# Window scan layer: two of the eight step-size products of a tile move from GpSimd to VectorE, with new order tables

## The reference

```python
dt = jax.nn.silu(dt_raw @ dt_W + dt_b)
a = -jnp.exp(A_log)
dA = jnp.exp(dt[..., None] * a)
dBx = dt[..., None] * b_st[:, :, None, :] * x[..., None]
def step(state, inp):
    dA_t, dBx_t, c_t = inp
    state = dA_t * state + dBx_t
    y = jnp.einsum('bcn,bn->bc', state, c_t)
```

## Time and profile before

| | us |
|---|---|
| median of three runs | 4724.54 |
| lowest and highest | 4721.48, 4733.52 |
| the profiled execution: time | 4733.78 |
| its span (first to last instruction) | 4732.0 |
| TensorE busy | 4400.7 (93%) |
| VectorE busy | 3875.3 (82%) |
| GpSimd busy | 3672.9 (78%) |
| ScalarE busy | 3347.4 (71%) |

### The profile page before, as it was taken

One profiled execution on the slowest core, in us unless ns is written; L12 is line 12 of the kernel. 1 busy time (PEld: TensorE's weight loads), 2 busy tenths in 40 slices (PEclk: granted clock), 3 DMA queues, 4 the chain that ended last, 5 costly groups with the idle time before them and its releaser, 6 DMA issues. The chain is left out here.

```text
span 4732.0 us, 79417 instructions
## 1 busy us (share of the span) xinstructions
PE 4400.7 (93%) x24320; PEld 3136.2 (66%) x24320; DVE 3875.3 (82%) x7295; ACT 3347.4 (71%) x5828; POOL 3672.9 (78%) x3476
## 2 busy tenths in 40 slices
PE   3799999999999999999998799999999999999998
PEld 2465656565656565656555478877778787878887
DVE  2899999999999999999999477777777777777775
ACT  3888898889898889888986255555555555555555
POOL 1989898989898989989898267766666676666666
PEclk7899999999999999999999799999999999999999
DMA  2011111111111111111111400031001300040000
GB/s 76 12 49 33 49 34 49 33 49 33 49 38 45 38 45 38 44 38 45 40 42 41 129 13 22 21 97 43 22 21 28 105 22 20 22 120 19 16 20 19
DMA packets 139268, 198.15 MB, mean 42 GB/s; under 512 B 18346, under 2 KB 106388, under 8 KB 138644
## 3 DMA queue, kind: packets, MB, share of 16 engines
q1 hardware_dynamic: 138900, 193.76, 12.9%
HBM read 114.02 MB, written 79.69 MB: 41 GB/s over the span
## 5 line engine op out<-in xcount | busy, mean ns | idle before, releaser
L1273 POOL TENSOR_TENSOR pl<-probs,ph 128x512 fp32r<-128x512 f32 x1024 | 1322.2, 1292 | 649.6 <-PE ps_o L1383 322.1
L742 POOL TENSOR_TENSOR dec<-dt,rates 128x384 f32<-128x384 f32 x1536 | 1512.9, 1015 | 285.2 <-ACT dt L628 229.6
L1476 ACT ACTIVATE ph<-ps_s 128x512 fp32r<-128x512 f32 x1024 | 612.7, 598 | 908.3 <-PE ps_s L1366 900.7
L1488 DVE TENSOR_REDUCE part_max<-ps_m 128x1 f32<-128x512 f32 x1024 | 687.4, 688 | 394.4 <-PE ps_m L1349 394.3
L1375 PE MATMUL ps_o<-ph,vh 128*128 128x512 f32 x2048 | 813.4, 397 | 17.6 <-ACT o_ch L1462 17.3
L1375 PE MATMUL ps_o<-ph,vl 128*128 128x512 f32 x2048 | 806.5, 394 | 0.0
L1517 DVE TENSOR_TENSOR ps_a<-probs,ps_a 128x512 f32<-128x512 f32 x992 | 681.3, 687 | 40.8 <-ACT probs L1478 35.3
L1383 PE MATMUL ps_o<-pl,vh 128*128 128x512 f32 x2048 | 635.1, 391 | 0.0
L1478 ACT ACTIVATE probs<-ps_s 128x512 f32<-128x512 f32 x1024 | 607.3, 593 | 0.0
L900 DVE SCALAR_TENSOR_TENSOR psS<-u,bc,psS 128x384 f32<-128x384 f32 x1024 | 597.3, 611 | 1.2
L909 DVE SCALAR_TENSOR_TENSOR y_tok<-psS,bc,y_tok 128x384 f32<-128x384 f32 x960 | 552.3, 604 | 4.5
(11 more groups left out here) (166 smaller groups left out, 7671.8 us busy)
## 6 DMA issues: line engine op xcount, KB each, us to landing
values_d<-hid SPq DMA_DIRECT2D x64, 512.0 KB, 4.3
xf<-in_x_dram SPq DMA_DIRECT2D x128, 128.0 KB
xb<-in_x_dram SPq DMA_DIRECT2D x128, 128.0 KB
residual_d<-xb SPq DMA_DIRECT2D x32, 512.0 KB, 2.6
vh<-values_d SPq DMA_DIRECT2D x32, 512.0 KB, 7.4
vl<-values_d SPq DMA_DIRECT2D x32, 512.0 KB, 9.1
res<-residual_d SPq DMA_DIRECT2D x32, 512.0 KB, 3.3
out_dram<-res SPq DMA_DIRECT2D x128, 128.0 KB
```

The lines of the kernel that those rows point to most:

```text
L742: last = nc.gpsimd.tensor_tensor(dec[:, q % RING, j - 1, :], dt[:, par, d, token_of(d, j), :], rates[:, d, n, :], ALU.mult)
L1273: nc.gpsimd.tensor_tensor(pl[:, m % DEPTH, :], probs[:, m % DEPTH, :], ph[:, m % DEPTH, :].bitcast(F32), ALU.subtract).then_inc(pl_ok, 1)
L1476: nc.scalar.activation(ph[:, m % DEPTH, :], ps_s[m % 2][:, :], ACT.Exp).then_inc(ph_ok, 1)
L1488: nc.vector.tensor_reduce(part_max[:, qt, kc:kc + 1], ps_m[r % 2][:, :], AX.X, ALU.max).then_inc(max_out, 1)
```

## The change

Three things. The products `umb2` and `umb3` are taken out of `POOL_ORDER` and put into `DVE_ORDER`, after st17 and after st22, where a new function `multiply` issues them as a tensor_tensor on VectorE. They count on a semaphore of their own, `u_dve`; `multiplied` counts GpSimd's six alone, and each reader of the backward products, and each step that overwrites an input, waits for both. And all four tables get a new order. Among what moves: on TensorE, out1 before conv0a, h2t0 before xnt0, w12 before pw2, inx2 to inx4 between w20 and w21, inx5 before dt2, the two x1t behind dt2, bct behind v1; on ScalarE, ow before exp2, z2 and exp4 before ln1_norm, exp6 before xnt0, inx1 and dt0 before exp12, exp0 to the end; on VectorE, w20 behind st35 and w21 behind st41; on GpSimd, acc13 before arg0, acc14 before umf3. The readers that are left out of the diff below change in the same way as those shown.

```diff
--- before.py
+++ after.py
@@ -38,26 +38,25 @@
 
 
 PE_ORDER = """
-    z0 z1 yt0- yt1- yt2- z2 out0- conv0a out1- conv1a conv2a conv0b conv0c conv1c conv2c xnt0+ h2t0- h2t1- xnt1+
-    pw0 w10- xnth+ pw1 w11- proj+ pw2 inx0+ w12- inx1+ w13- inx2+ dtf0+ dtb0+ w20- inx3+ w21- dtf1+ dtb1+ inx4+
-    x1t0- dtf2+ dtb2+ x1t1- inx5+ dtf3+ dtb3+ fg0- xk0+ xk1+ xk2+ v0- bct+ v1-
+    z0 z1 yt0- yt1- yt2- z2 out0- out1- conv0a conv1a conv2a conv0b conv0c conv1c conv2c h2t0- xnt0+ h2t1- xnt1+
+    pw0 xnth+ w10- pw1 w11- proj+ w12- pw2 inx0+ w13- inx1+ dtf0+ dtb0+ w20- inx2+ inx3+ inx4+ w21- dtf1+ dtb1+
+    inx5+ dtf2+ dtb2+ x1t0- x1t1- dtf3+ dtb3+ fg0- xk0+ xk1+ xk2+ v0- v1- bct+
 """.split()
 ACT_ORDER = """
-    exp1 ln1_std+ exp2 ow exp3 z0 z1 ln1_norm+ z2 exp4 ln2_std- exp5 ln2_norm- conv0c conv1c conv2c xnt0+ exp6
-    h2t0- h2t1- xnt1+ exp7 exp8 pw0 w10- xnth+ pw1 w11- exp9 proj+ exp10 pw2 inx0+ w12- inx1+ w13- exp11 inx2+
-    exp12 dtf0+ dtb0+ exp13 inx3+ exp14 dtf1+ dtb1+ inx4+ x1t0- dtf2+ dtb2+ x1t1- inx5+ dtf3+ dtb3+ exp15 fg0-
-    xk0+ xk1+ xk2+ exp0+ v0- bct+ v1-
+    exp1 ln1_std+ ow exp2 exp3 z0 z1 z2 exp4 ln1_norm+ ln2_std- exp5 ln2_norm- conv0c conv1c conv2c exp6 h2t0-
+    xnt0+ h2t1- xnt1+ exp7 exp8 pw0 xnth+ w10- pw1 w11- exp9 proj+ exp10 w12- pw2 inx0+ w13- exp11 inx1+ dtf0+
+    dtb0+ exp12 inx2+ inx3+ exp13 inx4+ exp14 dtf1+ dtb1+ inx5+ dtf2+ dtb2+ x1t0- x1t1- dtf3+ dtb3+ exp15 fg0-
+    xk0+ xk1+ xk2+ v0- v1- bct+ exp0+
 """.split()
 DVE_ORDER = """
-    st0 ln1_stats+ st1 ln1_mean+ st2 yt0- st3 yt1- st4 ln1_rstd+ st5 yt2- st6 ln1_shift+ st7 st8 st9 out0- st10
-    out1- ln2_stats- ln2_mean- st11 st12 ln2_rstd- st13 ln2_shift- st14 st15 st16 st17 st18 st19 st20 st21 st22
-    st23 st24 st25 st26 st27 st28 st29 st30 st31 st32 st33 st34 st35 st36 st37 st38 st39 w20- w21- st40 st41
-    st42 st43 st44 st45 fg0- st46 st47 gd_mul+ v0- gd_sum+ v1-
+    st0 ln1_stats+ st1 ln1_mean+ st2 yt0- st3 st4 ln1_rstd+ yt1- st5 yt2- st6 ln1_shift+ st7 st8 out0- st9 st10
+    out1- ln2_stats- ln2_mean- st11 st12 ln2_rstd- st13 ln2_shift- st14 st15 st16 st17 umb2 st18 st19 st20 st21
+    st22 umb3 st23 st24 st25 st26 st27 st28 st29 st30 st31 st32 st33 st34 st35 w20- st36 st37 st38 st39 st40
+    st41 w21- st42 st43 st44 st45 fg0- st46 st47 gd_mul+ v0- gd_sum+ v1-
 """.split()
 POOL_ORDER = """
-    arg2 arg3 umb0 acc0 arg4 acc1 arg5 umb1 umb2 acc2 arg6 acc3 arg7 acc4 arg8 umb3 acc5 arg9 acc6 arg10 acc7
-    arg11 acc8 arg12 acc9 arg13 acc10 arg14 acc11 arg15 acc12 arg0+ acc13 umf0+ umf1+ umf2+ umf3+ acc14 acc15
-    arg1+
+    arg2 arg3 acc0 arg4 acc1 umb0 arg5 umb1 acc2 arg6 acc3 arg7 acc4 arg8 acc5 arg9 acc6 arg10 acc7 arg11 acc8
+    arg12 acc9 arg13 acc10 arg14 acc11 arg15 acc12 acc13 arg0+ umf0+ umf1+ umf2+ acc14 umf3+ acc15 arg1+
 """.split()
 RATES_BEFORE = "proj"
 
@@ -196,9 +195,13 @@
     return state_op(k, q, op) if q >= 0 else state_op(k - 1, q + CHAINS, op)
 
 
-def multiplied(f, d, t):
-
-    return 2 * T * f + T * d + t + 1
+U_BY_DVE = [step for step, at in map(target, DVE_ORDER) if step.startswith("um")]
+U_BY_POOL = 2 * T - len(U_BY_DVE)
+
+
+def multiplied(f, d):
+
+    return U_BY_POOL * f + (T if d == 0 else U_BY_POOL)
 
 
 def token_of(d, j):
...
@@ -623,7 +627,9 @@
                 elif job.startswith("dt"):
                     d, t = "fb".index(job[2]), int(job[3])
                     if t == 0 and f > 1:
-                        act.wait_ge(u_mul, multiplied(f - 2, d, T - 1))
+                        act.wait_ge(u_mul, multiplied(f - 2, d))
+                        if d == 1:
+                            act.wait_ge(u_dve, len(U_BY_DVE) * (f - 1))
                         act.wait_ge(arg_ok, CHAINS * (f - 2) + STATES * (d + 1))
                     last = nc.scalar.activation(dt[:, par, d, t, :], bank[:, 0:INNER], ACT.Silu)
                 elif job.startswith("z"):
...
@@ -793,8 +800,19 @@
                                                           ALU.mult, ALU.mult)
                 last.then_inc(ok, 1)
 
+            def multiply(f, step, par):
+
+                d, t = "fb".index(step[2]), int(step[3])
+                dve.wait_ge(front_out, front_job(f, "dtb3"))
+                dve.wait_ge(front_out, front_job(f, "xk2"))
+                if f > 0:
+                    dve.wait_ge(state_ok, TILE_OPS * f)
+                nc.vector.tensor_tensor(u[:, d, t, :], dt[:, par, d, t, :], x_win[:, t, :], ALU.mult).then_inc(u_dve, 1)
+
             def front(step, f, par):
-                if step.startswith("ln1") and step != "ln1_std":
+                if step.startswith("um"):
+                    multiply(f, step, par)
+                elif step.startswith("ln1") and step != "ln1_std":
                     if step == "ln1_stats":
                         dve.wait_ge(x_loaded, 96 * (f + 1))
 
...
@@ -880,7 +899,9 @@
                             if not (exact(k) and k < 2):
                                 dve.wait_ge(back_full, back_job(k - 2, "yt2"))
                         if q % STATES == 0:
-                            dve.wait_ge(u_mul, multiplied(k, d, T - 1))
+                            dve.wait_ge(u_mul, multiplied(k, d))
+                            if d == 1:
+                                dve.wait_ge(u_dve, len(U_BY_DVE) * (k + 1))
                         dve.wait_ge(exp_ok, 2 * (CHAINS * k + q) + 1)
                         t0 = token_of(d, 0)
                         nc.vector.scalar_tensor_tensor(s_t, u[:, d, t0, :], scalar(q, t0, "b"), s_t,
```

More of the change, by code:

```diff
@@ L319, in layer0 @@
         u_mul = sem("u_mul")
+        u_dve = sem("u_dve")
         arg_ok = sem("arg_ok")
@@ L641, in front @@
                     if job == "xk0" and not (exact(f) and f == 0):
-                        act.wait_ge(u_mul, multiplied(f - 1, 1, T - 1))
+                        act.wait_ge(u_mul, multiplied(f - 1, 1))
+                        act.wait_ge(u_dve, len(U_BY_DVE) * f)
                     i = int(job[-1])
@@ L698, in own_terms @@
             def own_terms(k, par):
-                act.wait_ge(u_mul, multiplied(k, 0, T - 1))
+                act.wait_ge(u_mul, multiplied(k, 0))
                 act.wait_ge(direct_ok, 2 * k + 2)
```

## The result

| | us, median (lowest to highest, runs) |
|---|---|
| before | 4725.72 (4721.48 to 4733.52, 4) |
| changed | 4785.75 (4780.08 to 4793.46, 4) |
| ratio | 1.0119, 95% interval 1.0104 to 1.0134 |
| profiled execution of the changed kernel: time, span | 4780.08, 4778.3 |

The account below looks back on a forecast made before the run. No engine is full in layer 0; a ring of waits bounds it. 41.6 + 26.9 + 8.54 = 77.05 us plus 0.65 for clock drops gives 77.7 against 77.86 a tile, -5 us over 31 periods: 4720 us (4678 to 4766).

Parts of the forecast that it names:

- The ring: Layer 0: engines waiting for one another in a circle, taken to set the tile period; 77.05 us without a clock drop.
- The three links: Layer 0 tile: st0 to exp10 41.6 us, exp10 to exp15 26.9, exp15 to the next st0 8.54.
- The stall before dt2: TensorE waiting for banks ahead of the dt2 pair: to grow from 1.64 to some 2.3 us.
- the one before h2t0: TensorE idling ahead of h2t0: a second stall of some 1.8 us, which could add another 0.3.
- the waits before out1: TensorE's bank wait of 0.93 us ahead of out1: to be gone under the new order.
- Layer 1's work: Layer 1, from 2620 us, not touched by the change: to stay at 2112 us.
- GpSimd's wait for dt: GpSimd in layer 0: to wait near 6 us a tile for dt, 4.3 before for the last one.
- Link 1: VectorE's st0 to ScalarE's exp10: 41.6 us against 41.83, a gain of 0.2, with acc6 waiting for VectorE's z3(6).
- rival A: Clearly faster: no clock drop, 4700 us, or products at 0.46 us on VectorE, down to 4669; chance 0.38.
- the 36.92 us after st0 of the sum: VectorE's z3(6) start: moved from 34.78 us after st0 by 2.14 us for the two products.
- The clock: TensorE at half clock after the dt2 stall: half of the tiles losing about 1.3 us, 0.65 us a tile.
- Rival B: Slower by TensorE's clock: the drop behind dt2 in every tile, +1.6 us on 77.05, 4749 us; chance 0.21.

Follow-up runs that it names:

- after_fill8: Changed kernel plus 8 extra matmuls, whose result nobody reads, in each TensorE stall, before dt2 and before h2t0: 4711.72 us, ratio 0.9966.
- products_only: Kernel before with its four old order tables, only umb2 and umb3 moved to VectorE: 4705.55 us, ratio 0.995.
- after_fill8_h2t: Changed kernel plus 8 extra unread matmuls in the stall before h2t0 alone: 4773.99 us, ratio 1.0095.
- after_late_conv: Changed kernel with conv0a back before out1 and z2 back behind ln1_norm, no extra matmuls: 4775.85 us, ratio 1.01.
- after_x1t: Changed kernel with x1t0 put in front of dt2 on TensorE and ScalarE, no extra matmuls: 4730.53 us, ratio 1.0003.
- after_both: Changed kernel with x1t0 before dt2, conv0a back before out1 and z2 back behind ln1_norm, no extra matmuls: 4727.33 us, ratio 0.9994.
- after_fill8_dt: Changed kernel plus 8 extra unread matmuls in the stall before dt2 alone: 4725.67 us, ratio 0.9997.

## Why the prediction was wrong

*The ring.* The three links and their sum came out at a full clock: I had 41.6 + 26.9 + 8.54 = 77.05 us, and the tiles of `after_fill8` have 41.54 + 27.22 + 8.54 = 77.3. The stall before dt2 was to be some 2.3 us and is 1.94 to 2.08; the one before h2t0 was to be 1.8, which is its mean (17.6 us in 10), with 1.2 to 2.3 in single tiles; the waits before out1 went. Layer 1's work did not change. GpSimd's wait for dt was to be near 6 us a tile and was 2.1: it now waits first for VectorE's z3 and x_win.

*Link 1: right by luck.* A product was sized at 1.07 us from the own terms and measures 0.65 (median; 0.72 in `after_fill8`); the 0.46 of rival A was never seen, the shortest took 0.61. With products 0.4 us cheaper each, z3(6) should come 0.8 us earlier than the 36.92 us after st0 of the sum, and it does: at 36.12 in `after_fill8`. But exp10 comes no earlier. In the prediction acc6 waits for z3(6); in the trace z3(6) is done at 1538.70 and acc6 starts at 1539.43, when GpSimd, which has no wait behind acc3, gets to it. acc3 starts 24.7 us after st0 in the kernel before and in `after_fill8` alike, as it waits (0.25 us) for VectorE's z3(3); so what umb2 frees ahead of acc3 gains nothing. Behind acc3 only umb3 is gone, 1.0 us, and GpSimd pays 0.6 of it back, in the operations beside the two products: acc4 takes 1.33 us and not 1.00, the three exponents of arg9 3.23 and not 2.92. That is the 0.3 us of link 1. Rows of `after_fill8`: VectorE's st0 and z3(6); GpSimd's acc3, acc4, arg9, acc6; exp10 on ScalarE. The last row is acc3 of the kernel before, whose st0 is at 1512.34.

```profile
1501.98 0.60 DVE L915 SCALAR_TENSOR_TENSOR psS<-u,bc,psS 128x384 f32<-128x384 f32 x1
1538.10 0.60 DVE L919 SCALAR_TENSOR_TENSOR dec<-psS,bc,dec 128x384 f32<-128x384 f32 x1
...
1526.72 1.00 POOL L772 TENSOR_TENSOR y_tok<-y_tok,dec 128x384 f32<-128x384 f32 x1 [0.26 <-DVE dec L919]
1530.74 1.33 POOL L772 TENSOR_TENSOR y_tok<-y_tok,dec 128x384 f32<-128x384 f32 x1
1536.24 3.23 POOL L757 TENSOR_TENSOR dec<-dt,rates 128x384 f32<-128x384 f32 x3
1539.43 1.00 POOL L772 TENSOR_TENSOR y_tok<-y_tok,dec 128x384 f32<-128x384 f32 x1
...
1543.52 0.49 ACT L709 ACTIVATE psS<-dec 128x384 f32<-128x384 f32 x1
...
1537.03 1.00 POOL L757 TENSOR_TENSOR y_tok<-y_tok,dec 128x384 f32<-128x384 f32 x1 [0.25 <-DVE dec L890]
```

*The clock: the step that failed.* "I take half of the tiles: 0.65", at 1.3 us each. Instead the drop comes behind dt2 in 15 of 19 tiles, behind h2t0 in 13 of 20, and it is often longer. Its price a tile is (4785.75 - 4711.72) / 31 = 2.4 us: 1.9 at dt2 and 0.4 at h2t0 from the runs with one filler (60 and 12 us), where 0.65 and nothing stood. A drop at dt2 costs then 1.9 x 19 / 15 = 2.4 us, almost twice the 1.3 of the sum; the size was more wrong than the share. The trace gives the same: exp10 to exp15 takes 27.22 us at a full clock, 28.86 with a short drop (1.6 more) and 30.17 with a long one (3.0 more, and another 0.7 from exp15 to the next st0, 9.22 us where it was 8.54). Rival B named the mechanism and priced it at 1.6 us: that is the short drop, and it had no long ones, nor more than 0.3 for h2t0. With B at 2.4 the sum is 77.05 + 2.4 = 79.45, 49 us above before.

*Chances.* B had 0.21, although the prediction itself worked out that the stall would pass two microseconds in every tile. The drop came in 8 of 20 tiles behind stalls that were all 1.64 us long. So stalls of this length already brought the lower clock, and nothing in the trace said how fast the share would grow with a longer one; I took it for a share to be nudged.

## What to carry to other kernels

A stall of TensorE has two prices: its own, which may be nothing off the critical path, and the half clock of the work that follows it. Where some tiles of a kernel show the lower clock behind one particular stall, a reordering that lengthens it by three or four tenths of a microsecond can cost more than all it gains elsewhere, and a small piece of real work moved into it can win most of that back. Test each half of a combined change alone: here two products with the old tables were the whole gain, over half of it because the stall before dt2 shrank and the clock no longer fell, and the new tables were the loss. And check a sum that comes out right term by term: link 1 did, on a path that was not the one that bound it.

## What the runs showed of the hardware that was not expected

- How the drop goes with the stall before dt2: with 1.41 to 1.43 us none in 20 tiles (`products_only`), with 1.64 in 8 of 20 (before), with 1.94 to 2.08 in 15 of 19 (changed), with 2.07 in 19 of 19 (`after_fill8_h2t`, and `after_late_conv`); 1.3 to 1.4 us and up to 0.31 more, with 0.5 us of transposes between them, in 5 of 20 (`after_x1t`) and 8 of 20 (`after_both`).
- The length does not decide alone. Before h2t0, stalls of 2.2 to 2.3 us had a drop in all 13 tiles of the changed kernel that had them, and in 10 of 20 in `after_fill8_dt`. What else decides, no run here shows.
- Adding work makes the kernel faster: 16 records of unused matmuls in each of two stalls (1.95 us each) took 1.5% off the changed kernel, and 12 in one stall took 0.3% off the one before. The same trick twice as large cost 0.4% on the kernel before.
- A tensor_tensor on VectorE with both inputs in SBUF, beside a busy GpSimd, took 0.62 to 0.82 us in the changed kernel, and 0.63 to 1.18 (median 0.80) in `products_only`, where it stands elsewhere against GpSimd's work; the own terms fell from a median of 1215 to 722 ns there.
- The fastest version of all runs is `products_only`, 0.5% under the kernel before.
